# Second cross attention: the mask's parts enter the key product, one exponential takes two key blocks, and the bias tile goes

## The reference, cut to what matters

```python
x = x + _L1_xattn_ref(ctx_2048, _layernorm(x, axis=-1), mask_BxS2_ik0, L1_xattn_b)

def _L1_xattn_ref(memory, query, seq_mask, b):          # H = 8 heads, depth 16
    Q = _split_heads(query, H) * depth ** (-0.5)
    k_mem, v_mem = jnp.split(memory, 2, axis=2)
    K, V = _split_heads(k_mem, H), _split_heads(v_mem, H)
    logits = jnp.einsum('bhqd,bhkd->bhqk', Q, K) + b[0]
    logits = logits + -1e+30 * (1.0 - mask)             # mask: 1 for a key that counts
    weights = jax.nn.softmax(logits, axis=-1)
    out = jnp.einsum('bhqk,bhkd->bhqd', weights, V)
```

## Time and profile before

| | us |
|---|---|
| median of three runs (lowest, highest) | 4383.67 (4382.56, 4385.84) |
| profiled execution: span from the first to the last instruction | 4381.2 |
| median of the runs less this span | 2.5 |
| `cross1`: layer norm begins, last addition ends | 1182.6 to 1692.0 |
| `cross1`: exponentials, first to last | 1302.0 to 1680.3 |

### The profile page before, as it was taken

One profiled execution on the slowest core, in us unless ns is written; L12 is line 12 of the kernel. 1 busy time (PEld: TensorE's weight loads), 2 busy tenths in 40 slices (PEclk: granted clock), 3 DMA queues, 4 the chain that ended last, 5 costly groups with the idle time before them and its releaser, 6 DMA issues. The chain is left out here.

```text
span 4381.2 us, 72541 instructions
## 1 busy us (share of the span) xinstructions
PE 3735.4 (85%) x28025; PEld 2217.6 (51%) x28030; DVE 2959.0 (68%) x4913; ACT 2383.6 (54%) x4244; POOL 1543.0 (35%) x1271
## 2 busy tenths in 40 slices
PE   3299999989829997699779999999999999999654
PEld 2133333358703333467446666666666666666442
DVE  3399999944427773655437777777777777777747
ACT  3188888853319896222216656666656566666330
POOL 0200000000040000322006667766666777676410
PEclk6599999989959998799789999999999999999877
DMA  5322222100044540000010000000000000000000
GB/s 174 67 45 45 51 49 48 31 17 17 13 72 77 82 63 2 29 2 2 9 60 1 16 1 16 1 16 1 16 1 16 1 16 1 1 1 1 7 30 24
DMA packets 119911, 123.02 MB, mean 28 GB/s; under 512 B 21200, under 2 KB 97840, under 8 KB 119184
## 3 DMA queue, kind: packets, MB, share of 16 engines
q1 hardware_dynamic: 119432, 117.95, 12.2%
q10 hardware_dynamic: 144, 0.52, 0.0%
HBM read 102.56 MB, written 15.73 MB: 27 GB/s over the span
## 5 line engine op out<-in xcount | busy, mean ns | idle before, releaser
L831 DVE TENSOR_REDUCE att_peak.1<-psS 128x1 f32<-128x512 f32 (+1 forms) x1024 | 580.3, 631 | 95.7 <-PE psS L701 95.6
L2191 POOL TENSOR_TENSOR key_sums_0.1<-key_sums_0.1,prob_0.1 128x512 f32<-128x512 f32 x256 | 440.4, 1720 | 28.7 <-POOL key_sums_0.1 L2191 0.4
L2191 POOL TENSOR_TENSOR key_sums_1.1<-key_sums_1.1,prob_1.1 128x512 f32<-128x512 f32 x256 | 420.1, 1641 | 28.7 <-POOL key_sums_1.1 L2186 0.4
L800 ACT ACTIVATE att_probT.1<-psT 128x512 f32<-128x512 f32 (+1 forms) x682 | 368.7, 568 | 75.0 <-PE psT L730 33.5
L831 DVE TENSOR_REDUCE att_peak.2<-psS 128x1 f32<-128x512 f32 (+1 forms) x512 | 266.5, 568 | 139.6 <-PE psS L701 137.9
L2100 DVE TENSOR_TENSOR att_highest.1<-att_highest.1,prob_0.1 128x1024 f32<-128x1024 f32 (+1 forms) x160 | 273.2, 1708 | 128.3 <-ACT prob_0.1 L2035 121.3
L2100 DVE TENSOR_TENSOR att_highest.1<-att_highest.1,prob_1.1 128x1024 f32<-128x1024 f32 (+1 forms) x160 | 279.3, 1745 | 114.5 <-ACT prob_1.1 L2035 107.7
L701 PE MATMUL psS<-key_stack.1,query_stack.1 64*128 64x512 bf16 (+1 forms) x1024 | 271.6, 386 | 94.8 <-DMA key_stack.1<-key_parts 48.2
L747 PE MATMUL psM<-att_probT.1,quad_values.1 128*9 128x256 f32 (+1 forms) x3840 | 306.3, 391 | 19.5 <-issue 19.5
L2121 DVE TENSOR_TENSOR prob_0.1<-prob_0.1,psO 128x1024 f32<-128x1024 f32 (+1 forms) x256 | 243.7, 1013 | 49.0 <-PE psO L1951 49.0
L2121 DVE TENSOR_TENSOR prob_1.1<-prob_1.1,psO 128x1024 f32<-128x1024 f32 (+1 forms) x256 | 243.7, 1013 | 49.1 <-PE psO L1951 49.1
(11 more groups left out here) (696 smaller groups left out, 8070.2 us busy)
## 6 DMA issues: line engine op xcount, KB each, us to landing
key_stack.1<-key_parts SPq DMA_DIRECT2D x384, 58.0 KB
key_stack.2<-key_parts SPq DMA_DIRECT2D x96, 200.1 KB
ctx_rows.1<-in_ctx_dram SPq DMA_DIRECT2D x8, 1536.0 KB
key_parts<-split_parts.1 SPq DMA_DIRECT2D x8, 1200.8 KB, 5.6
ctx_keys_0.1<-in_ctx_dram SPq DMA_DIRECT2D x4, 768.0 KB
ctx_keys_1.1<-in_ctx_dram SPq DMA_DIRECT2D x4, 768.0 KB
query_stack.1<-query_parts SPq DMA_DIRECT2D x192, 16.0 KB
ctx_values_0.1<-in_ctx_dram SPq DMA_DIRECT2D x4, 768.0 KB
```

Source lines behind the costliest of these rows:

```text
L800: last = self.k.nc.scalar.activation(probs[:, blks[0]:blks[-1] + 1, :].rearrange("p b q -> p (b q)"), bank[0:w, 0:len(blks) * S], ACT.Exp)
L831: self.k.nc.vector.tensor_reduce(self.peak[:, 2 * h + s, c:c + 1], self.score_bank[m % 3][:, 0:w], AX_X, ALU.max).then_inc(self.peak_done. ...
L2191: nc.gpsimd.tensor_tensor(acc, acc, own[:, h, c * BANK:(c + 1) * BANK], ALU.add).then_inc(self.summed.sem, 1)
```

## The change

`key_rows` now takes rows 0 to 101 where there is a mask, so the key product adds the mask's three parts times one, as the score product does. The exponential needs no bias: each bin takes one exponential of 512 columns, as in `cross0`. The bias tile, its loads, its flags, the 13 transposes, the two copies, the memset and the store of `key_bias` are gone. No shape of a matmul changes but the contraction, 99 to 102 rows.

```diff
     def key_rows(self, h):
-        return slice(64 * h, 64 * h + 64) if self.halves else slice(0, 99)
+        return slice(64 * h, 64 * h + 64) if self.halves else slice(0, 102 if self.masked else 99)
...
         load_context(k, sp, crows[b % 2], b, self.ctx_loaded[b % 2], slice(D, DC))
-        if self.masked:
-            if b >= 2:
-                sp.wait_ge(*self.exp_done(2 * self.NB * (self.heads // 2) * (b - 1)))
-            sp.dma_start(self.bias[:, b % 2, :], k.key_bias[b, :, :]).then_inc(self.bias_loaded[b % 2].sem, 16)
...
-        if self.masked and i == 0 and g % (self.heads // 2) == 0:
-            b = g // (self.heads // 2)
-            act.wait_ge(*self.bias_loaded[b % 2](16 * (b // 2 + 1)))
         for h in range(2):
             m = 2 * (g * self.NB + i) + h
             act.wait_ge(*self.turned(m + 1))
             bank, probs = self.key_bank[m % 3], self.probT[0:w, g % self.RING, h]
-            if not self.masked:
-                last = self.k.nc.scalar.activation(probs[:, blks[0]:blks[-1] + 1, :].rearrange("p b q -> p (b q)"), bank[0:w, 0:len(blks) * S], ACT.Exp)
-            for n, blk in enumerate(blks if self.masked else ()):
-                bias = self.bias[0:w, g // (self.heads // 2) % 2, blk:blk + 1]
-                last = self.k.nc.scalar.activation(probs[:, blk, :], bank[0:w, n * S:(n + 1) * S], ACT.Exp, bias=bias)
-            last.then_inc(self.exp_done.sem, 1)
+            self.k.nc.scalar.activation(probs[:, blks[0]:blks[-1] + 1, :].rearrange("p b q -> p (b q)"), bank[0:w, 0:len(blks) * S],
+                                        ACT.Exp).then_inc(self.exp_done.sem, 1)
...
-                link(nc.vector.memset(maskT[:], 0.0))
...
-                dve.wait_ge(*turned(1))
-                byblock = k.psM[:, 0:KB * B].rearrange("p (t b) -> p b t", b=B)
-                link(nc.vector.tensor_copy(maskT[:, :, 0:KB - 1], byblock[:, :, 0:KB - 1]))
-                nc.vector.tensor_copy(maskT[0:KTAIL, :, KB - 1], byblock[0:KTAIL, :, KB - 1]).then_inc(made.sem, 1)
...
-                for t in range(KB):
-                    w = P if t < KB - 1 else KTAIL
-                    last = nc.tensor.transpose(k.psM[0:w, t * B:(t + 1) * B], mask[:, t * P:t * P + w], k.ident[0:B, 0:B])
...
-                sp.dma_start(k.key_bias.rearrange("b p t -> p b t"), maskT[:]).then_inc(stored.sem, 16)
                 sp.dma_start(k.mask_parts, parts[:]).then_inc(stored.sem, 16)
```

More of the change, by code:

```diff
@@ L496, in __init__ @@
         self.ctx_loaded = [k.flag(f"ctx_loaded_{i}") for i in range(2)]
-        self.bias_loaded = [k.flag(f"mask_loaded_{i}") for i in range(2)] if masked else None
     def finish(self):
@@ L521, in finish @@
             sig.passed(32 * (B // 2))
-        if self.masked:
-            for sig in self.bias_loaded:
-                sig.passed(16 * (B // 2))
     def parts(self, h):
@@ L984, in mask_by_key @@
     nc = k.nc
-    chain, turned, made, stored = k.flag("dve_chain"), k.flag("mask_turned"), k.flag("mask_made"), k.flag("stored")
-    scaled = k.flag("mask_scaled")
+    chain, made, stored = k.flag("dve_chain"), k.flag("mask_made"), k.flag("stored")
     with ExitStack() as own:
@@ L989, in mask_by_key @@
         parts = k.sb("mask_parts", [B, 3, KC], BF16, ctx=own)
-        maskT = k.sb("mask_by_key", [P, B, KB], ctx=own)
         with nc.Block() as block:
@@ L994, in _ @@
                 link = Chain(dve, chain)
-                link(nc.vector.memset(maskT[:], 0.0))
                 link(nc.vector.tensor_scalar(mask[:], flags[:], 1.0, -MASKED, ALU.subtract, ALU.mult))
-                nc.vector.tensor_scalar(mask[:], mask[:], shift[0:B, 0:1], None, ALU.add).then_inc(scaled.sem, 1)
-                dve.wait_ge(*scaled(1))
+                link(nc.vector.tensor_scalar(mask[:], mask[:], shift[0:B, 0:1], None, ALU.add))
                 link(nc.vector.tensor_copy(parts[:, 0, :], mask[:]))
@@ L1001, in _ @@
                 link(nc.vector.tensor_copy(parts[:, 1, :], rest[:]))
-                link(nc.vector.tensor_tensor(parts[:, 2, :], rest[:], parts[:, 1, :], ALU.subtract))
-                dve.wait_ge(*turned(1))
-                byblock = k.psM[:, 0:KB * B].rearrange("p (t b) -> p b t", b=B)
-                link(nc.vector.tensor_copy(maskT[:, :, 0:KB - 1], byblock[:, :, 0:KB - 1]))
-                nc.vector.tensor_copy(maskT[0:KTAIL, :, KB - 1], byblock[0:KTAIL, :, KB - 1]).then_inc(made.sem, 1)
-                link.end()
-            @block.tensor
-            def _(pe):
-                pe.wait_ge(*scaled(1))
-                for t in range(KB):
-                    w = P if t < KB - 1 else KTAIL
-                    last = nc.tensor.transpose(k.psM[0:w, t * B:(t + 1) * B], mask[:, t * P:t * P + w], k.ident[0:B, 0:B])
-                last.then_inc(turned.sem, 1)
+                nc.vector.tensor_tensor(parts[:, 2, :], rest[:], parts[:, 1, :], ALU.subtract).then_inc(made.sem, 1)
+                link.end()
             @block.sync
@@ L1019, in _ @@
                 sp.wait_ge(*made(1))
-                sp.dma_start(k.key_bias.rearrange("b p t -> p b t"), maskT[:]).then_inc(stored.sem, 16)
                 sp.dma_start(k.mask_parts, parts[:]).then_inc(stored.sem, 16)
-                sp.wait_ge(*stored(32))
-    for sig in (turned, made, scaled):
-        sig.passed(1)
-    stored.passed(32)
+                sp.wait_ge(*stored(16))
+    made.passed(1)
+    stored.passed(16)
 def cross1(k):
```

4 lines of the change are left out of this document (removed).

## The result

The changed kernel took 4349.8 us (median of 4 runs, 4346.1 to 4352.3) beside 4383.8 for the kernel before on the same chip (4382.6 to 4385.8): ratio 0.9924, interval 0.9912 to 0.9937. That is 34 us, or 0.8%, faster. The forecast was 4355, range 4347 to 4367. The profiled spans are 4350.5 and 4381.2 us, so these two traces account for 30.7.

A forecast was written before the change was run, and what follows sets the result against it. TensorE was taken to bound `cross1`, with ScalarE in balance and mattering only where TensorE waits. Terms 6.6 + 8.0 + 6.7 + 2.3 + 4.1 + 1.1 = 28.8 off 4381.2 gave 4352.4, with 2.5 around it 4355; range 4347 to 4367.

The forecast's parts named there:

- The mechanism: In `cross1`, cheaper ScalarE work pays only where TensorE waits for it; 28.8 us in all, chance 0.63.
- wide slots: Rival: ScalarE also bounds TensorE's 512-key slots in `cross1`, which shrink from 1.53 to some 1.36; 4330 us, chance 0.04.
- TensorE's direct waits for VectorE: Rival: VectorE takes over in `cross1`'s score loop, so gains at narrow slots and start fall away; 4363.8 us, chance 0.10.
- no fall was left: Rival: the clock keeps falling behind the shorter stalls at `cross1`'s 14 hand-overs; five falls stay, 4361.6 us, chance 0.20.
- the first two terms: The gains forecast for `cross1`'s narrow slots, 6.6 us, and its quad hand-overs, 8.0 us.
- Narrow slot: Key products after a narrow score step in `cross1` go from 0.75 to 0.53, in 30 pairs: 6.6 us.
- Hand-over: TensorE's stall ahead of block 0's values, between quads, falls from 1.53 to about 0.96, 14 times: 8.0 us.
- Clock: With stalls of 0.96, none of five falls to 1.2 GHz behind `cross1`'s quad changes remains, 1.33 each: 6.7 us.
- Start: In `cross1`'s first pairs TensorE's waits for exponentials shrink: 2.3 us, range 0 to 4.
- End: In `cross1`'s last pairs, without scores, values come every 1.1 instead of 1.46, and the last copies sooner: 4.1 us.
- Mask: The separate stage preparing the mask loses DVE's copies, memset and one store: 1.1 us, range 0 to 2.
- Queue and rows at nothing: Dropping eight bias loads from SP's queue gains 0; contracting 102 rows instead of 99 loses between 0 and 1 us.

The follow-up runs named there:

- The late copy: The changed kernel with ScalarE's copy of the sums moved behind bin 6's exponentials, in `cross1` alone: 4372.7 us, ratio 0.9979.
- the run with 99: The changed kernel with the key product back to 99 rows, the mask left out of the probabilities: 4350.6 us, ratio 0.9930.

## Why the prediction was right, step by step

The mechanism held: a lighter ScalarE pays where TensorE waits for it, and the clock stops falling at the hand-overs. The rivals are out: wide slots stayed at 1.53, TensorE's direct waits for VectorE stayed small (4.0 us in 16, before 3.3 in 15), and no fall was left between 1302 and 1657 us in the changed kernel's trace. The sum came out 4.6 short of the 33.4 measured. That it came so near is in part luck: the first two terms together were 1.3 too high, while 3.1 for the table load, 2.3 for two more clock falls and 1.3 for the odd wait stood in no term.

1. *Narrow slot*: right, 0.75 to 0.53.
2. *Hand-over*: right in kind, 0.49 instead of 0.57 a time, 6.9 instead of 8.0. The mis-sized term is the start of bin 5's exponentials. I let them start at the end of the third key product, 1511.07, which is 0.49 behind the start of the first (1510.58). They start 0.58 behind it (1470.09 to 1470.67), 0.09 later. The wait left is 1.15, not 0.96, for that reason and a second one: the last key product of the narrow bin started 0.19 behind the one before it, now it starts 0.11 behind and ends 0.11 sooner after the narrow bin's start, so TensorE is at the hand-over earlier.
3. *Clock*: all five falls gone, 6.6 of 6.7. Against the number of falls stand the waits at this place of `cross1`: at 1.15 none of 70 (five traces), at 1.28 none of 14, at 1.53 five of 14, at 1.69 nine of 14, and with no such wait none. The late copy changed nothing but this wait, and the falls came back; that is shown, and so is their price of 1.33. That 0.96 would be short enough was a bet, as the trace before could not decide it: in `cross0` the clock falls 13 times behind hand-over waits of 0.64 that have one of 0.53 ahead of them. So the length of one wait tells something only between stages that are otherwise alike. Why some waits of one length have a fall behind them and others not stays open; the counts at 1.53 and 1.69 are of one trace each. The Trainium skill ("TensorE: Matmul & The Clock Gate", "HAM oscillation — how this bites in real kernels") names as the cause idle gaps longer than all of these waits. By it the falls would have had another cause and stayed. The late copy's nine falls behind waits of 1.69, and the 13 in `cross0` behind waits of 0.53 and 0.64, speak against it here.
4. *Start*: 2.3 forecast, 5.5 measured. The exponentials' share was 1.8. Missed were the clock fall at 1319.14 (0.55 in these two pairs) and, with 3.1, the removed wait itself: I asked what the bias load's wait delayed (nothing), and not which instruction carries the other wait once there are two. The row was there to see: 1300.71, 3.01 idle, behind the key product.
5. *End*: 4.1 forecast, 4.9 measured, but for another reason in part: 1.6 of it is the clock fall at 1680.95, which was in no term. What the lighter ScalarE gives is 3.3, 0.8 less than forecast: values every 1.14 (1.1 forecast) and the last hand-over give 2.7, and the last pair's step to it another 0.6.
6. *Mask*: 1.1 forecast, 1.9 in this pair of traces, 10.91 against 12.79 to 13.00 in all. I had counted the engines' work and the issue of the store, and these came as forecast. The other 0.8 lie behind them: from the start of the last store to the next step it takes 3.84 before (1203.06 to 1206.90) and 3.08 after (1202.01 to 1205.09). The transfers of 1202 to 1207 us before and 1201 to 1206 after give the likely reason:

```profile
DMA packets 1056, 0.13 MB, mean 26 GB/s; under 512 B 1048, under 2 KB 1048, under 8 KB 1048
```

```profile
DMA packets 16, 0.08 MB, mean 15 GB/s; under 512 B 8, under 2 KB 8, under 8 KB 8
```

The bias went out as over a thousand small packets, and the barrier waited for them. No run takes the store alone away, so this split is argued.

7. *Queue and rows at nothing*: right for the rows (the run with 99). The loads ahead of the first scores vary by about a microsecond from run to run, so nothing can be read there.

The odd wait of 1.16 (1.3 us) was not in the sum; it comes and goes with a late instruction fetch, and no run shows that this hangs on the edit. With the scatter of later stages (here -2.7), the profile's 30.7 and the medians' 34.0 and 33.1 agree with the account.

## What to carry to other kernels

When a helper engine gets cheaper, look in the waiting engine's timeline for the instruction that is waited for, and what is queued ahead of it on the helper. Here one copy stood behind the exponentials of a bin and two row copies, none of which TensorE needed as early as the copy: moving it by one slot in the kernel before gave 24 us, and the whole change, with 84 us less work, 34. Count a removed or added wait by where the compiler puts it, not only by its length: a second wait ahead of an activation moved a table load onto the path and, with the clock, cost 3 us. And count a clock fall wherever it stands: in every stage of the trace, not only behind the wait that you mean to shorten.

## What the runs showed of the hardware

- The granted clock fell to 1.2 GHz for 3.4 us behind single waits of 1.53 us (five of 14) and 1.69 us (nine of 14, one of them for 6.8 us) in a TensorE stage more than 90% busy, and each fall of 3.4 us there cost 1.33 us; behind single waits of 1.15 and 1.28 us it never did there.
- It also fell behind short waits that stand close together: 13 times in `cross0` behind 0.53 and 0.64, and once in `cross1` behind 0.41, 0.45 and 0.41.
- While TensorE starts a stage at 1.2 GHz, a single extra wait of 0.75 us delayed full clock from 7 to 15 us after the first row product.
- The bias operand of one column cost an exponential of 256 columns 0.09 us (0.48 against 0.39); doubling the columns to 512 costs 0.20 (0.594). The Trainium skill ("ScalarE: Activation LUTs", "What ACT_TABLE_LOAD costs") gives such an operand the same 0.09; the trace agrees.
- 99 or 102 contraction rows made no difference to the key product (a quad of 22.46 against 22.43 us).
